# The end of the last batch: who adds x and the heavy rows to the light rows, and in which sequence norm, casts and finals run

## What is computed

```python
h = _layernorm(x) * (1 + ca) + sa
# light path: every token
attn = softmax(einsum(qw * scale, look_around(k)))      # windows of 64, three at a time
light_out = merge(einsum(attn, look_around(v))) @ wo_l
# heavy path: 256 tokens chosen by a router score, written back to their places
heavy_out = zeros_like(x).at[batch, iq].set(ho)
x = x + ga * (light_out + heavy_out)
h = _layernorm(x) * (1 + cb) + sb
hid = square(relu(einsum('bsd,fd->bsf', h, W_fc)))
y = einsum('bsf,df->bsd', hid, W_proj)
# five steps: mem = 0.9 * mem + y - reset; spike where mem > 1
x = x + gb * (sum of spikes) / 5
```

## Time and profile before

| | us |
|---|---|
| median of 3 runs | 909.43 |
| lowest and highest | 908.33, 911.7 |
| the profiled execution's own time | 910.43 |
| its span | 908.5 |

### The profile page before, as it was taken

One profiled execution on the slowest core, in us unless ns is written; L12 is line 12 of the kernel. 1 busy time (PEld: TensorE's weight loads), 2 busy tenths in 40 slices (PEclk: granted clock), 3 DMA queues, 4 the chain that ended last, 5 costly groups with the idle time before them and its releaser, 6 DMA issues.

```text
span 908.5 us, 23925 instructions
## 1 busy us (share of the span) xinstructions
PE 832.5 (92%) x9170; PEld 634.2 (70%) x9170; DVE 587.2 (65%) x1738; ACT 612.5 (67%) x1738; POOL 212.9 (23%) x271
## 2 busy tenths in 40 slices
PE   4769789999999999999999999999999999899766
PEld 2446567678776787678776887678776877677566
DVE  6746663786568756776568746875668646533645
ACT  2157566688667876788567876788578776688333
POOL 3311221120230224221331114222222022100433
PEclk8789779999999999999999999999999999999878
DMA  9401030120022001300022002200031001200100
GB/s 318 135 24 31 1 101 13 43 71 2 26 70 83 25 14 53 112 25 2 25 79 75 25 14 76 89 25 9 24 99 49 25 18 37 89 1 2 47 18 24
DMA packets 32847, 45.35 MB, mean 50 GB/s; under 512 B 3304, under 2 KB 28144, under 8 KB 32512
## 3 DMA queue, kind: packets, MB, share of 16 engines
q1 hardware_dynamic: 29616, 37.53, 12.6%
q0 software_dynamic: 2304, 6.29, 2.3%
q10 hardware_dynamic: 816, 0.00, 0.0%
HBM read 32.52 MB, written 14.97 MB: 52 GB/s over the span
## 4 chain that ended last, share of the span: by engine, by line
PE 76%; DVE 11%; ACT 6%; issue 3%; DMA 2%; POOL 1%; SPq 1%; DVEq 0%; POOLq 0%; ACTq 0%
PE ps_unit L1003 30%; PE ps_y L1125 10%; PE ps_turned L1176 6%; PE ps_unit L1052 5%; PE ps_scores L1150 5%; PE ps_turned L1196 4%; PE ps_turned L1211 4%; PE ps_unit L1057 3%; PE ps_scores L1159 3%; ACT probs L937 2%; DVE hn L1414 1%; DMA late<-in_L_wmod 1%; DVE loT L1456 1%; PE ps_turned L1201 1%; PE ps_unit L1082 1%
## 5 line engine op out<-in xcount | busy, mean ns | idle before, releaser
L937 ACT ACTIVATE probs<-ps_scores,row_min 128x192 f32<-128x192 f32 (+2 forms) x384 | 160.8, 424 | 104.7 <-DVE row_min L1439 58.2
L947 ACT ACTIVATE probs<-probs,row_inv 128x192 f32<-128x192 f32 (+2 forms) x384 | 155.5, 456 | 0.0
L1439 DVE TENSOR_REDUCE row_min<-ps_scores 128x2 f32<-128x512 f32 (+1 forms) x128 | 78.6, 614 | 58.8 <-PE ps_scores L1150 28.6
L1176 PEld LDWEIGHTS ps_turned<-ident,probs 64*128 64x128 f32 x1280 | 56.1, 139 | 81.3 <-issue 73.3
L1003 PE MATMUL ps_unit<-xT,wqkv 128*128 128x512 f32 x384 | 109.6, 424 | 3.3 <-POOL xT L755 3.3
L1176 PE MATMUL ps_turned<-ident,probs 64*128 64x64 f32 x1280 | 81.7, 239 | 27.4 <-DVE loT L1456 25.1
L1125 PE MATMUL ps_y<-wprojT,hid_parts 128*128 128x256 f32 x768 | 104.6, 285 | 0.3
L1125 PEld LDWEIGHTS ps_y<-wprojT,hid_parts 128*128 128x128 f32 x768 | 97.2, 189 | 8.3 <-issue 4.0
L1003 PEld LDWEIGHTS ps_unit<-xT,wqkv 128*128 128x128 f32 x384 | 71.7, 196 | 32.1 <-issue 18.1
L1003 PE MATMUL ps_unit<-h_parts,wfcT 128*128 128x512 f32 x336 | 89.9, 403 | 0.0
L955 ACT ACTIVATE probsT<-ps_turned 128x384 f32<-128x384 f32 x128 | 61.8, 483 | 26.3 <-PE ps_turned L1201 25.9
(11 more groups left out here) (175 smaller groups left out, 1657.0 us busy)
## 6 DMA issues: line engine op xcount, KB each, us to landing
xa<-in_L_attn_x SPq DMA_DIRECT2D x8, 512.0 KB, 4.4
normed_rows<-hn SPq DMA_DIRECT2D x8, 512.0 KB, 3.0
lx<-in_L_attn_x SPq DMA_DIRECT2D x8, 512.0 KB, 3.8
out_x<-spikes SPq DMA_DIRECT2D x16, 256.0 KB, 2.2
hn<-routed_out SPq DMA_DIRECT2D x7, 512.0 KB, 4.0
routed_out<-zero_rows SPq DMA_DIRECT2D x14, 256.0 KB, 4.1
full<-mod_rows SPq DMA_DIRECT2D x7, 256.0 KB
gate_a<-mod_rows SPq DMA_DIRECT2D x8, 128.0 KB, 3.9
```

The costliest lines, as they stand in the source:

```text
L937: ins = act.activation(probs[:, probs_buffer(n), probs_columns(s, part)], ps_scores[:, part, lo:hi], ACT.Exp, bias=row_min[:, n % 3, part: ...
L947: ins = act.activation(rows, rows, ACT.Identity, scale=row_inv[:, n % 3, part:part + 1])
L1176: ins = pe.transpose(ps_pT[:, c, i * W:(i + 1) * W], probs[rows, probs_buffer(n), run * P:(run + 1) * P], ident[rows, rows])
L1439: ins = dve.tensor_reduce(row_min[:, n % 3, :], ps_scores[:, :, lo:hi], AX.X, ALU.min)
```

## The change

Five things are altered, all but the last in the last batch.

1. GpSimd adds the heavy rows to x at slot 22 (`join_rows`), in two adds of 128x512, as soon as both are loaded. It no longer adds light rows tile by tile there; the light rows are added by VectorE's `add_rows`, which now reads `lx` and `lg_last`.
2. VectorE: `copy_out` of the last slot stands ahead of `third_norm` of the first half; the casts of the first half stand ahead of `add_rows` and `stats3` of the second; the casts of the second half stand behind `FC` 3's square.
3. GpSimd: `rstd3` of the first half stands ahead of the second `final`, which now waits until the first half's norm is done (`z3_ready`); `rstd3` of the second half stands behind the square of `FC` 0.
4. TensorE: `FC` 3 and `YA` 1 stand ahead of `Z3` 2 and 3.
5. The first product that reads new normalised rows (`FC` 0, in the tail also `FC` 8) waits for each of its two depths by itself. This one is in every batch.

```diff
-    23: ["y15"],
+    23: ["y15", "add_half", "stats_half"],
 }
-LAST_POOL_SLOTS = {"gather": 2, "rstd3": 7, "tail_gather": 19}
+LAST_POOL_SLOTS = {"gather": 2, "rstd3": 7, "tail_gather": 19, "join": 22}
...
     "tail": [("LX", 2), ("LX", 3), ("Z3", 0), ("Z3", 1), ("FC", 0), ("FC", 1), ("FC", 2), ("YA", 0),
-             ("Z3", 2), ("Z3", 3)]
-            + [u for i in range(3, 2 * FT) for u in (("FC", i), ("YA", i - 2))]
+             ("FC", 3), ("YA", 1), ("Z3", 2), ("Z3", 3)]
+            + [u for i in range(4, 2 * FT) for u in (("FC", i), ("YA", i - 2))]
...
+            def join_rows(n):
+
+                pool.wait_ge(lx_loaded, 16 * n + 16)
+                for half in range(2):
+                    pool.wait_ge(*((tail_loaded, 16) if half else (spread_loaded, 16 * n + 16)))
+                    ts = slice(half_tiles(half).start, half_tiles(half).stop)
+                    pool.tensor_tensor(lx[:, ts, :], lx[:, ts, :], gathered[:, ts, :], ALU.add).then_inc(lx_ready, 1)
...
+                if last:
+                    rstd3(b, 0)
+                    pool.wait_ge(z3_ready, b + 1)
                 if not first:
                     final(pool, b - 1, 1)
...
-            rstd3(B - 1, 0)
-            add_x("tail", B, ("LX", 2))
-            add_x("tail", B, ("LX", 3))
-            rstd3(B - 1, 1)
             for u in SEGMENTS["tail"]:
-                if u[0] != "LX":
-                    unit("tail", B, u)
+                unit("tail", B, u)
+                if u == ("FC", 0):
+                    rstd3(B - 1, 1)
...
                 for k in range(KD):
+                    if made is not None:
+                        pe.wait_ge(h2_high, made + k + 1)
+                        pe.wait_ge(h2_low, made + k + 1)
...
-                    if i == 0:
-                        pe.wait_ge(h2_high, 2 * b)
-                        pe.wait_ge(h2_low, 2 * b)
-                    if i == FT:
-                        pe.wait_ge(h2_high, 2 * b + KD)
-                        pe.wait_ge(h2_low, 2 * b + KD)
+                    made = KD * (b - 1 + i // FT) if i % FT == 0 else None
...
-            add_rows(B - 1, 0)
-            stats3(B - 1, 0)
             copy_out(SLOTS * B - 2, slot_at(SLOTS - 2, True))
             unit("tail", B, ("LX", 2))
+            copy_out(SLOTS * B - 1, slot_at(SLOTS - 1, True))
             third_norm(B - 1, 0)
-            copy_out(SLOTS * B - 1, slot_at(SLOTS - 1, True))
             unit("tail", B, ("LX", 3))
+            for i in range(KD):
+                high_part("tail", B, ("Z3", i))
             add_rows(B - 1, 1)
             stats3(B - 1, 1)
-            for i in range(KD):
-                high_part("tail", B, ("Z3", i))
             for i in range(1, FT, 2):
                 square_low(dve, B, i)
                 if i == 1:
                     third_norm(B - 1, 1)
+                if i == 3:
                     for j in range(KD, 2 * KD):
                         high_part("tail", B, ("Z3", j))
```

More of the change, by code:

```diff
@@ L758, in add_x @@
             def add_x(segment, b, u):
-                kind, t = u
+                _, t = u
                 n = light_batch(segment, b, u)
-                rows = lg_last[:, t, :] if kind == "LX" else lg[:, t % 2, :]
                 pool.wait_ge(lx_loaded, 16 * n + 16)
                 wait_drained(pool, segment, b, u)
-                pool.tensor_tensor(lx[:, t, :], lx[:, t, :], rows, ALU.add).then_inc(lx_ready, 1)
+                pool.tensor_tensor(lx[:, t, :], lx[:, t, :], lg[:, t % 2, :], ALU.add).then_inc(lx_ready, 1)
+            def join_rows(n):
[4 more added lines that the diff above has]
+                    pool.tensor_tensor(lx[:, ts, :], lx[:, ts, :], gathered[:, ts, :], ALU.add).then_inc(lx_ready, 1)
             def unit(segment, b, u):
@@ L773, in unit @@
                     low_part(segment, b, i)
-                elif kind in ("LO", "LX"):
+                elif kind == "LO":
                     add_x(segment, b, u)
@@ L789, in iteration @@
                         spread(segment, b, b, "HX")
+                    if last and s == at["join"]:
+                        join_rows(b)
                     if not last:
@@ L996, in fill, with split_product @@
                 return ps_unit[bank], filled[bank]
-            def split_product(ps, w, w_cols, a, a_cols):
+            def split_product(ps, w, w_cols, a, a_cols, made=None):
                 n = 0
                 for k in range(KD):
+                    if made is not None:
+                        pe.wait_ge(h2_high, made + k + 1)
+                        pe.wait_ge(h2_low, made + k + 1)
                     for wi, ai in ((0, 0), (0, 1), (1, 0)):
@@ L1102, in unit @@
                 elif kind == "FC":
-                    if i == 0:
-                        pe.wait_ge(h2_high, 2 * b)
-                        pe.wait_ge(h2_low, 2 * b)
-                    if i == FT:
-                        pe.wait_ge(h2_high, 2 * b + KD)
-                        pe.wait_ge(h2_low, 2 * b + KD)
+                    made = KD * (b - 1 + i // FT) if i % FT == 0 else None
                     f, cols = chunk_tokens(segment, i)
                     ins = split_product(ps[:, cols], lambda p, k, cc: wfcT[p][:, k, cc], slice(f * P, f * P + P),
-                                        lambda p, k, cc: h2T(segment)[p][:, k, cc], cols)
+                                        lambda p, k, cc: h2T(segment)[p][:, k, cc], cols, made)
                 ins.then_inc(full_bank, 1)
@@ L1379, in add_rows @@
             def add_rows(n, half=None):
-                dve.wait_ge(lx_ready, T * n + half_tiles(half).stop)
+                ts = slice(half_tiles(half).start, half_tiles(half).stop)
                 if half is None:
+                    dve.wait_ge(lx_ready, T * n + T)
                     dve.wait_ge(spread_loaded, 16 * n + 16)
-                elif half == 0:
-                    dve.wait_ge(spread_loaded, 16 * n + 16)
-                else:
-                    dve.wait_ge(tail_loaded, 16)
-                if half is None:
-                    dve.wait_ge(final_ready, 2 * n + 1)
-                ts = slice(half_tiles(half).start, half_tiles(half).stop)
-                dve.tensor_tensor(x2_rows(n)[:, ts, :], lx[:, ts, :], gathered[:, ts, :], ALU.add).then_inc(x2_ready, 1)
+                    dve.wait_ge(final_ready, 2 * n + 1)
+                    rows = gathered
+                else:
+                    dve.wait_ge(lx_ready, T * n + half + 1)
+                    if half == 0:
+                        wait_drained(dve, "last", n, ("LX", 0), ("LX", 1))
+                    else:
+                        wait_drained(dve, "tail", B, ("LX", 2), ("LX", 3))
+                    rows = lg_last
+                dve.tensor_tensor(x2_rows(n)[:, ts, :], lx[:, ts, :], rows[:, ts, :], ALU.add).then_inc(x2_ready, 1)
             def stats3(n, half=None, tiles=None):
@@ L1535, in stages @@
                         third_norm(b - 1)
+                    elif name == "add_half":
+                        add_rows(b, 0)
+                    elif name == "stats_half":
+                        stats3(b, 0)
                     elif name[0] == "y" and not first:
```

## The result

| | before | after |
|---|---|---|
| median | 909.42 us (6 runs) | 903.42 us (6 runs) |
| lowest and highest | 907.49, 911.7 | 902.07, 905.02 |
| profiled execution (its span) | 910.43 (908.5) | 903.56 (901.6) |

The medians lie 6.0 us apart. The ratio of the runs is put at 0.9927 with a 95% interval of 0.9912 to 0.9943, which is 5.2 to 8.0 us less: beyond the 0.5% mark. The prediction said 901.1 (899.5 to 904.6). Between the two profiled executions it is 6.9 us; the prediction's sum for the same pair was 8.3.

The account below looks back on a forecast made before the run. TensorE was taken as the bound, with waits in the last batch's end delaying `FC` 4. Gains 2.7 + 1.35 + (7.15 - 4.05) + 1.35, less 0.2, make 8.3 us: 902.1 profiled, 901.1 median, range 899.5 to 904.6.

Parts of the forecast that it names:

- Rival A: Clock falls once in the new end, `FC` 0 to part of `FC` 3 slow: costs 1.2 to 2.8 us; chance 0.23.
- Rival B: Second half's norm late for the transposes ahead of `FC` 4, VectorE and GpSimd lengthening each other: up to 1.2 us; chance 0.10.
- Joins: GpSimd's two early adds of heavy rows to x in the last batch: end near 852, cost 0, covered by idle time.
- First add: VectorE's first add in the tail: 0.70 us instead of 1.10 with GpSimd idle; rstd by 862.0 instead of 863.7.
- Copy ahead of norm: VectorE's last slot copy before the first half's third norm: light product 3 starts at 862.65, not 865.35, 2.7 us.
- Light product 3: TensorE's last light product: full clock after a shorter stop, 1.99 us instead of 3.36, gaining 1.35.
- To `FC` 0: Gate multiply to `FC` 0: adds and statistics leave the path, first cast collides with `final` (0.3 us); cumulative gain 7.15 us.
- `FC` 0 to `FC` 4: Tail on TensorE at full clock: 0.6 us stop before `YA` 0, `FC` 4 at 872.9 against 881.44; adds 1.35 us.
- slack 0.4: Second half's norm in the tail: ends at 871.5, 0.4 us before TensorE needs it, the plan's thinnest margin.
- Split waits elsewhere: Two more waits at `FC` 0 in each of seven other batches: cost taken as 0.2 us, between near 0 and 2.0.
- from `FC` 4 on the end is at a fixed distance: Alternating `FC` and `YA` without gaps: `FC` 4 to the end is 27.1 us, so its earlier start is time saved.
- Rivals C and D: C: little changes, half clock from light product 3, 906.6 us, chance 0.07. D: slower, clock stays low, up to 919.6, chance 0.03.

Follow-up runs that it names:

- e9: Changed kernel without the joins: GpSimd adds light rows to x tile by tile again, VectorE the heavy ones; 900.29 us, ratio to before 0.9965.
- e4: Changed kernel with the split wait of `FC` 0 kept in the tail alone, old single wait in the other seven batches; 903.7 us, ratio to before 0.9947.
- e1: Kernel before with one edit, VectorE's `copy_out` of the last slot ahead of the first half's third norm; 906.78 us, ratio 0.9972.
- e3: Changed kernel plus unread filler matmuls on TensorE, 8 behind the first half's transposes and 4 behind `FC` 2; 903.39 us, ratio to before 0.9938.
- e2: Kernel before plus unread filler matmuls, 22 ahead of light product 3 and 28 behind the first half's transposes; 909.46 us, ratio 1.000.
- e10: Changed kernel with second-half transposes apart and later, their casts moved, and the previous batch's last `final` split behind `FC` 4 and `FC` 6; 902.87 us, ratio to before 0.9925.
- e11: Changed kernel run again, unaltered, in a later group; 903.54 us, ratio to before 0.993.
- group 1: First of three groups of runs, each beside its own runs of the kernel before, whose median here was 909.33 us.
- Group 2: Second of three groups of runs, without a run of the changed kernel itself; its kernel before had median 904.14 us.

## Why the prediction was right, and where it was not

The direction and the place were right: all of the gain is between light product 2 and `FC` 4. The size was too large, by 1.4 of 8.3 us in the profiled pair and by 2.3 in the median (903.42 for 901.1). The time fell where rivals A and B end, not where the forecast's own story does; the range held it because it had been drawn to cover them.

1. *Joins.* Right that they are free: they end at 851.9, forecast 852. What they bring was told too narrowly (a shorter first add): e9 says 0.8 us, at the casts.
2. *First add* 0.68, forecast 0.70. Rstd ends at 862.26, forecast 862.0.
3. *Copy ahead of norm.* 2.76 for 2.7; timed alone 2.5.
4. *Light product 3* 1.97, forecast 1.99, in all traces of the changed order but e4. e1 shows that it is not the short stop alone that keeps the clock.
5. *To `FC` 0.* Two pieces, as forecast, the first at 866.92 (forecast 866.7, with all starts 0.1 later). The first cast took 0.74 and not 0.53: the `final` beside it ended at 866.16 and not 865.8, the cast 0.15 after it, as forecast. By undoing: collision 0.35 to 0.45, split wait 0.4 to 0.5.
6. *`FC` 0 to `FC` 4.* **This step failed**, at the sentence on the second half's norm, "slack 0.4", and in the full clock that it assumed. At full clock e3 has rstd ready 8.8 us after light product 3, forecast 8.15: GpSimd's remainder of `FC` 0 took 1.00 beside VectorE's square of `FC` 1, and `FC` 0 came 0.1 later. Then the norm took 1.45, forecast 0.73. So it ends 10.3 us after light product 3, not 8.85. Take off the slack, and `FC` 4 is 1.1 us late, of the 1.2 that are missing. Part of this had already shown as a longer stop ahead of `YA` 0: from `FC` 0 to `YA` 0 the forecast has 2.95, e4 3.65. Rival B had the mechanism and the size (up to 1.2); what it did not see is that the norm itself collides, with `FC` 2's square and remainder.
7. *Split waits elsewhere.* Not settled.

Last, "from `FC` 4 on the end is at a fixed distance" held within 0.1 us when both ends are read in one view: 27.22 before and 27.30 after. The prediction's 27.1 is 0.16 short of the timeline because it took the chain's start of `FC` 4. The 0.08 are there because `FC` 4 is now the first product behind the transposes, so that the next one starts 0.82 after it and not 0.71; a distance from a landmark is fixed only if that landmark keeps its neighbours.

Rival A came true in the profile (half clock from 868.4 to 871.4), and there TensorE's slow products are what came last ahead of the transposes. It is still not the cause by itself: its price, taken from product durations in before, ignored that the remainder and the norm would have stopped TensorE in the same place (e3, e4). Nor is B by itself, since in the profile of the changed kernel the norm was done 0.66 us early. Together A and B give what one of them gives. Rivals C and D found nothing: the clock was full again by 871.8.

## What to carry to other kernels

Before a slow stretch is priced, ask which wait stands right behind it: in `FC` 0 to 2, e3 gave TensorE 0.9 us back and e2 1.8, and that bought 0.0 and 0.6. Where a late operand can't come earlier, put its consumer behind more independent work (`FC` 3 and `YA` 1: 1.3 us; two more pairs, which also hide ScalarE's work behind the transposes: 0.7 to 1.3). And when GpSimd work is moved, look at what VectorE does at the new time: two adds of 128x512 cost nothing at 849 us, two smaller ones 0.8 beside the casts.

## What the runs showed of the hardware

**VectorE and GpSimd lengthen each other's instructions, both ways.** VectorE's norm took 0.73 alone and 1.45 beside GpSimd's square and subtract; its remainder 0.42 alone, 0.77 and 1.40 beside them; its cast 0.29 alone, 0.74 beside a `final`. GpSimd's subtract took 0.73 alone and 1.00 beside VectorE's square. Which of the two is lengthened went by who started first: in e3 VectorE's square of `FC` 1 started 0.02 us ahead of GpSimd's subtract of `FC` 0 (0.43 and 1.00), in the changed kernel 0.35 behind it (0.66 and 0.73). The Trainium skill, "SBUF — State Buffer", section "Who interferes with whom", says that such VectorE operations share a pair of ports with GpSimd and that whoever issues first has it for the whole instruction. The traces agree in the order and in the ends: in e3 the norm ended 0.16 us after GpSimd's subtract, in e10 the remainder 0.29 after the multiply. That the ports are the reason no run here shows. Two such pairs, the remainder of `FC` 0 and the second half's norm, are what step 6 was short by.

**The same code runs at different clocks from one execution to the next.** Light products 0 and 1 together took 3.72 us in six of the fourteen traces, 5.3 in two and 6.05 to 6.23 in the others; light product 2 took 1.99 or 2.87 to 3.48. (The granted clock was 0.53 from 849.7 to 855.0 in the changed kernel, where the two took 6.15, and 1.00 from 851.6 to 855.3 in e11, where they took 3.72.) The three together differ by at most 1.5 us (6.7 to 8.2), so they do not explain the spread of the whole: 4 to 8 us in the kernel before (904.8 to 912.9 in group 1), as much as this change is worth, and 1 to 6 us in the others. Group 2's kernel before was also 5 us faster than that of group 1 on the same chip (904.14 for 909.33); why is open.
